# A decoder layer on one core: where each pair of heads is mixed with its values, and into which bank

## The reference, cut to what matters

```
x = layernorm(x + attention(x) @ Wo)        # 8 x 112 tokens, 1024 features, 16 heads of 64
x = layernorm(x + cross_attention(x, ctx))  # 8 x 375 context tokens, one head of 1024
x = layernorm(x + x @ W.T + bias + lora(x))

attention:  q, k, v = x @ Wq, x @ Wk, x @ Wv
            q, k = rotary(q), rotary(k)
            logits = q @ k.T / 8, masked to be causal
            out = softmax(logits) @ v       # "mixing the heads", the part that the change moves
```

## Time and profile before

| | |
|---|---|
| median of 3 executions | 577.46 us (573.81 to 579.15) |
| the profiled execution | 578.72 us, its span 576.7 us |
| mean granted clock of TensorE | 0.994 of full speed |
| PE busy | 559.1 us, 97% of the span |
| ScalarE, GpSimd, VectorE busy | 221.0, 216.0 and 209.4 us |
| matmuls of the projections, line 407 | 3 x 384 |
| matmuls of the heads, line 458 | 256, in 16 blocks |

### The profile page before, as it was taken

How to read it: one execution, slowest core, us unless ns; L and a number is a source line. 1 busy time by engine, 2 the same in 40 slices (tenths; PEclk the granted TensorE clock), 3 DMA queues, 4 the chain that set the end, 5 groups by cost and what they waited for, 6 DMA issues and landing times.

```text
span 576.7 us, 7991 instructions
## 1 busy us (share of the span) xinstructions
PE 559.1 (97%) x3112; PEld 468.3 (81%) x3112; DVE 209.4 (36%) x462; ACT 221.0 (38%) x531; POOL 216.0 (37%) x175
## 2 busy tenths in 40 slices
PE   7899999999999999999999999999979999999995
PEld 3798998889988899888888888778767576878784
DVE  5712405124052250522622543325453542442321
ACT  4314425235252352533545344144643353433220
POOL 3343525134251342511055555053972754420100
PEclk9899999999999999999999999999999999999998
DMA  8512102121021210500009946769737552651001
GB/s 330 192 37 74 38 0 74 38 73 38 2 74 36 74 38 1 183 1 1 1 13 296 226 117 181 188 201 281 222 115 222 159 161 74 210 175 43 0 38 73
DMA packets 22678, 62.00 MB, mean 108 GB/s; under 512 B 3257, under 2 KB 4409, under 8 KB 22641
## 3 DMA queue, kind: packets, MB, share of 16 engines
q1 hardware_dynamic: 22096, 61.32, 35.1%
q10 hardware_dynamic: 544, 0.18, 0.2%
HBM read 54.14 MB, written 3.67 MB: 100 GB/s over the span
## 4 chain that ended last, share of the span: by engine, by line
PE 87%; POOL 5%; DVE 3%; DMA 2%; ACT 1%; issue 1%; SPq 0%; POOLq 0%; ACTq 0%; DVEq 0%
PE bank L407 41%; PE bank L564 22%; PE bank L657 6%; PE bank L632 4%; PE bank L428 3%; PE bank L458 3%; PE bank L447 2%; POOL cf_lo L1431 2%; POOL ffn L1454 2%; DMA cf_raw<-ctx_feat 1%; PE bank L420 1%; DVE t_both L1291 1%; DMA w_raw<-qkv_w 1%; PE bank L609 1%; PE bank L677 1%
## 5 line engine op out<-in xcount | busy, mean ns | idle before, releaser
L407 PE MATMUL bank<-x_hi,w_hi 128*128 128x448 f32 x384 | 145.4, 379 | 4.5 <-DVE x_lo L1106 4.5
L407 PE MATMUL bank<-x_lo,w_hi 128*128 128x448 f32 x384 | 141.1, 367 | 0.0
L407 PE MATMUL bank<-x_hi,w_lo 128*128 128x448 f32 x384 | 140.8, 367 | 0.0
L407 PEld LDWEIGHTS bank<-x_hi,w_hi 128*128 128x128 f32 x384 | 72.5, 189 | 13.8 <-DVE x_lo L1106 3.4
L407 PEld LDWEIGHTS bank<-x_hi,w_lo 128*128 128x128 f32 x384 | 72.6, 189 | 6.0
L407 PEld LDWEIGHTS bank<-x_lo,w_hi 128*128 128x128 f32 x384 | 72.7, 189 | 5.1
L1397 POOL TENSOR_TENSOR w_lo<-w_mix,w_hi 128x1024 fp32r<-128x1024 f32 x15 | 38.2, 2549 | 88.9 <-ACT w_hi L781 87.7
L1431 POOL TENSOR_TENSOR cf_lo<-cf_raw,cf_hi 128x752 fp32r<-128x752 f32 x32 | 56.9, 1800 | 38.1 <-ACT cf_hi L899 38.1
L564 PE MATMUL bank<-ffn,act_hi 128*128 128x512 f32 x224 | 71.0, 398 | 0.0
L564 PE MATMUL bank<-wo,act_hi 128*128 128x512 f32 x224 | 69.7, 393 | 0.0
L800 ACT ACTIVATE prob<-prob,shift 112x112 f32<-112x112 f32 x128 | 47.9, 376 | 42.4 <-DVE shift L1154 42.4
(11 more groups left out here) (112 smaller groups left out, 831.4 us busy)
## 6 DMA issues: line engine op xcount, KB each, us to landing
w_raw<-qkv_w SPq DMA_DIRECT2D x24, 512.0 KB, 3.4
cf_raw<-ctx_feat SPq DMA_DIRECT2D x32, 376.0 KB, 5.8
ctx_tok<-ctx_tok SPq DMA_DIRECT2D x24, 448.0 KB
half_raw<-ffn_w SPq DMA_DIRECT2D x16, 256.0 KB, 4.2
x_raw<-x_feat SPq DMA_DIRECT2D x8, 448.0 KB, 8.1
out<-y_t SPq DMA_DIRECT2D x6, 512.0 KB, 2.6
wo_raw<-wo_w SPq DMA_DIRECT2D x8, 256.0 KB, 5.6
half_raw<-wo_w SPq DMA_DIRECT2D x8, 256.0 KB, 6.5
```

The costliest lines, as they stand in the source:

```text
L407: last = pe.matmul(to[:, 0:HT], a[:, k, :], b[:, k, HT * h:HT * h + HT], start=(k == 0 and b is x_hi and a is w_hi[w]), stop=(k == KT - 1 ...
```

## The change

For pairs 0 to 5, both halves of the heads are mixed next to each other, behind the projection of the values of the first half. The first half still goes to bank 6; the second goes to bank 7. ScalarE's `round_heads(p, 0)` moves behind `keep_v(s, 0)`, and both readers take the second half from bank 7. The count of `heads_rest` that is waited for becomes 2p - 1 for the first half; for the second it stays 2p + 1. For pairs 6 and 7 bank, order and counts stay as they were.

```
+        def heads_bank(p, r):
+
+            return bank[7] if r and p < last_p else HEADS
...
             def mix_heads(p, r):
                 pe.wait_ge(prob_t_kept, 4 * p + 2 * r + 2)
                 pe.wait_ge(v_tok_kept, 2 * p + r + 1)
-                if any_yet(2 * p + r):
-                    pe.wait_ge(heads_rest, 2 * p + r)
+                before = 2 * p + r if r or p >= last_p else 2 * p - 1
+                if any_yet(before):
+                    pe.wait_ge(heads_rest, before)
                 for b in range(HB):
                     for h in range(2):
-                        last = pe.matmul(HEADS[HD * h:HD * h + HD, b * S:(b + 1) * S],
+                        last = pe.matmul(heads_bank(p, r)[HD * h:HD * h + HD, b * S:(b + 1) * S],
...
                 project(1, 1, PROD[1])
-                mix_heads(p, 0)
                 turn_prob(p, 1)
                 pe.wait_ge(w_rest, 3 * (s - 1) + 3)
                 pe.wait_ge(qk_kept, 4 * s + 3)
                 project(2, 0, PROD[0])
+                mix_heads(p, 0)
                 mix_heads(p, 1)
...
             def round_heads(p, r):
                 act.wait_ge(heads_done, 2 * p + r + 1)
-                act.activation(act_hi[:, p, HT * r:HT * r + HT], HEADS[:, 0:HT],
+                act.activation(act_hi[:, p, HT * r:HT * r + HT], heads_bank(p, r)[:, 0:HT],
...
                 round_w(s + 1, 1)
-                round_heads(p, 0)
                 keep_prob_t(p, 1)
                 keep_v(s, 0, 6 * s + 5, PROD[0])
+                round_heads(p, 0)
                 round_heads(p, 1)
...
             def rest_heads(p, r):
                 dve.wait_ge(heads_rounded, 2 * p + r + 1)
-                dve.tensor_tensor(act_lo[:, p, HT * r:HT * r + HT], HEADS[:, 0:HT],
+                dve.tensor_tensor(act_lo[:, p, HT * r:HT * r + HT], heads_bank(p, r)[:, 0:HT],
```

## The result

The changed kernel takes 585.81 us (median of 6 executions, 585.28 to 587.38), the kernel before 576.23 us (6 executions). The ratio is 1.0168, with a 95% interval of 1.0136 to 1.0199: slower by 9.7 us, between 7.8 and 11.5. The profiled execution took 585.57 us, its span is 583.6 us at a granted clock of 0.992. The numbers of instructions are the same; PE is busy for 558.6 us, which is no more than before. The time has gone into standing still.

A forecast was written before the change was run, and what follows sets the result against it. TensorE bounds the kernel, busy 279.88 of 280 us. Per step + 1.30 (wait) + 0.08 (standstill) - 0.14 (transposes) = + 1.24 us; six steps add 7.4 to 577.46, giving 584.9 us, 8-in-10 range 581.0 to 588.5.

The forecast's parts named there:

- The count decides: Second half's mixing, pairs 0 to 5: still waiting for 2p + 1, it waits for the first half's rest; six waits.
- The size of one wait: Between the two mixings: 1.25 us through ScalarE and VectorE plus TensorE's restart, 1.30 us, between 1.29 and 1.39.
- The restart: TensorE starting again behind VectorE's rest: taken as 0.05 us, with 0.14 us kept for the range.
- The low end of 1.29 us for the wait: Lower bound of each wait between the two mixings, used in the low sum of 6.9 us for six steps.
- The block from a standstill: Second half's mixing, started after the wait: 1.00 us against 0.92 in the chain, a loss of 0.08 us.
- the transposes at 0.77 us: Second block of transposes in a step, now behind a projection: 0.77 us for 0.91, a gain of 0.14 us.
- What was costed at nothing: In the six steps: keep_v ahead of the rounding, earlier transposes, VectorE's readiness and bank 7 add no time.
- The sum: Six attention steps at + 1.24 us each: + 7.4 us, between 6.9 and 9.8, giving 584.9 us, 1.3% slower.
- the wait costs nothing: Rival: second mixing let go at once, - 0.29 us a step, - 1.7 us in all, 575.7 us; chance 4%.
- the delay would be taken back after the attention: Rival: TensorE's waits after 320 us shrink, returning up to 5.7 of 7.4 us, giving 579.2 us; chance 8%.
- the 1 us that the prediction allowed: From the attention's end to the kernel's end, the length should be as before within 1 us.
- the rival: Clock falls behind each new wait in the attention: 9 us on top for six, 593.9 us; chance 4%.

The follow-up runs named there:

- e1: The change with the second half in pairs 0 to 5 waiting for heads_rest 2p instead of 2p + 1; ratio 0.999 to the kernel before.
- e7: The change with count 2p + 1 kept only for second halves of pairs 3 to 5, pairs 0 to 2 waiting for 2p; ratio 1.0047 to the kernel before.
- e3: The change's order alone: both halves in bank 6, with the counts 2p and 2p + 1 of before; ratio 1.0145 to the kernel before.
- e4: The change with the second half waiting for ScalarE's rounding and heads_rest 2p, not VectorE's rest of the first half; ratio 1.0095 to the kernel before.
- e2: The kernel before with only second halves of pairs 0 to 5 moved to bank 7, order and counts unchanged; ratio 1.0018 to the kernel before.
- e0: The unaltered change timed once more beside the kernel before on the same chip; ratio 1.0157.
- e6: The change with four more ScalarE copies of the first half ahead of its rounding in pairs 0 to 5; ratio 1.0461 to the kernel before.

## Why the prediction was right, by its own steps

**The count decides.** Right. Six waits, from the end of the first half's mixing to the end of its rest, released by line 1176. e1 and e7 take them away one count at a time; e3 shows that the bank has no part in it.

**The size of one wait.** The way through ScalarE and VectorE was foreseen as 1.25 us and took 111.80 - 110.56 = 1.24. The restart was the mis-sized term: 0.14 us, not 0.05, which is + 0.09 x 6 = 0.5 us. The reason given for 0.05, a stream of matmuls behind a plain subtraction, does not hold. The start of the changed kernel has the same projection matmuls, released by the same subtractions, with both values:

```profile
L1111 DVE TENSOR_TENSOR x_lo<-x_raw,x_hi x2: 2149/2160/2170, 8.2 to 10.3; 128x896 fp32r<-128x896 f32 x2
10.49 0.44 PE L411 MATMUL bank<-x_hi,w_hi 128*128 128x448 f32 x1 [2.74 <-DVE x_lo L1111]
```

The first subtraction starts at 8.20 and ends at 10.35, and TensorE starts 0.14 us behind it; the next two restarts, at 12.50 and 16.05, come 0.05 to 0.06 us behind the end of theirs. Neither is it the engine: in the cross attention line 662 starts at 459.39, 0.05 us behind ScalarE's copy, and pair 0 of e4 starts 0.14 us behind ScalarE. What goes along with it at the start is the list: the first restart has two waits in front of it, for the weights and for x, the other two have one; the mixing has three. That isn't the whole rule, as the list has several waits in front of line 662 too, and only e4 varied it. The low end of 1.29 us for the wait is not worked out in the prediction; 1.37 lies inside its bounds. The block from a standstill, 0.99 us, and the transposes at 0.77 us were as foreseen; the first mixing took 0.94 for 0.92. Per step + 1.33 for + 1.24, in all 8.0 us for 7.4.

**What was costed at nothing** was nothing: keep_v ahead of the rounding (0.39 us to spare), the earlier transposes (no wait at line 451), VectorE idle in time, bank 7 (e2).

**The sum against the measurement.** The time came out 0.9 us from the forecast, 585.81 for 584.9, and a part of that is luck: the median of the kernel before had come down from 577.46 to 576.23 us with three more executions, which hid half of what the sum was short by. The + 7.4 us themselves lie just below the interval of the ratio, 7.8 to 11.5. The ratio says + 9.7 us, e0 + 9.1, e3 + 8.4; the steps say + 8.0, and less the clock the executions say + 7.5 and + 8.4. The rest of the first ratio lies within its interval. It isn't the clock behind the new waits, as far as profiles show: in the three profiles of kernels with waits of 1.4 us (the change, e0, e3), none of the 18 steps was longer than 37.46 us.

**The rivals.** That the wait costs nothing is e1, to the letter: steps shorter by 0.29 us. It needed the count 2p. There TensorE mixes into bank 7 while ScalarE reads bank 6, which no trace showed when the prediction was made. That the delay would be taken back after the attention is refuted for all but a small part: from the start of the output projection's long run to the end of the span, the change has 583.6 - 323.05 = 260.55 us and the kernel before 576.7 - 317.40 = 259.30. These 1.25 us more are outside the 1 us that the prediction allowed. They are, within 0.1 us, the fall of the clock in the cross attention, + 1.70, less a load of context that the chain waits for 0.5 us less, 6.88 us for 7.39; in e0 it is 6.94, and in the second profile of the kernel before 7.70. The clock did not fall behind waits of 1.4 us, as predicted; but the rival was a matter of length and not of kind. It came true in one of six waits of 1.8 us and in five of six of 3.1 us, and cost 1.6 to 2.9 us each time. The Trainium skill (TensorE: Matmul & The Clock Gate, "A second HAM failure mode: psum-queue depth-cycling") was named beside it for short idle times between groups of matmuls that make the clock swing. In the change they didn't, in any of its six steps. In e6 the clock does swing, but behind single waits of 3.1 us; whether the page means such waits it doesn't say.

## What to carry to other kernels

A second buffer saves nothing until the count that guards it is worked out anew: write down for each write which read frees that very buffer, and compare it with the number in the wait. When two users of a chain through other engines are moved next to each other, look at what lay between them, for it was the cover: the price of the uncovered way can be read from the trace of before, as end of the first to end of the last reader, plus the restart. A gain of 0.3% that the chain shows can disappear in what the clock varies by, and so a version with shorter steps isn't yet a kernel that is measured to be faster.

## What the runs showed of the hardware that was not expected

- TensorE starts 0.14 us after the end of the instruction that releases it in some places and 0.05 us after it in others, and both values occur behind VectorE and behind ScalarE. One more wait in the list behind the one that holds, though its count is long reached, goes with 0.10 to 0.14 us more: 0.14 us in pair 0 of e4, 0.24 to 0.28 us in pairs 1 to 5.
- The granted clock differs between executions of one kernel: the 23 executions of before beside e0 had means of 0.985 to 0.999. By the reckoning of the table a clock lower by 0.01 is 5.8 us of the span. The fastest of the 23 took 574.23 us at 0.999, the two at 0.985 took 580.41 and 580.48: 1.1% with the same program.
- A stretch at half clock follows single waits of TensorE of 1.8 us sometimes and of 3 us mostly, and was not seen in 21 steps with waits of 1.4 us (the change, e0, e3 and e7). In the cross attention it followed 7 of 11 waits of 2.2 to 3.2 us, in twelve profiles; one of 3.2 us was among those without it. So the length of the wait alone doesn't decide it.
